# Row maxima and attention output turned by VectorE in 32x32 blocks, and a third bank for the scores

## The chip, the cores and the metric

The kernel runs on one core of a Trainium2 chip. The metric is the device time of one execution in microseconds; before the change it is 676.68 us, the median of 3 runs (676.61 to 677.33). The core has TensorE (PE in the rows), VectorE (DVE), ScalarE (ACT), GpSimd (POOL) and SyncE (SP). Each has its own instruction stream and waits on semaphores; DMAs are issued from the streams of SyncE (SPq) and ScalarE (ACTq).

## The reference

The input is x, 8 images of 16 by 16 tokens with 192 channels, float32. It goes through two transformer blocks with window attention and then two Fourier blocks. The two attention blocks differ in weights, in epsilon and in the Gelu's name only:

```
h = layernorm(x)
win = window_partition(pad(h), 14)            # a 16x16 image becomes 4 windows of 196 tokens, three of them mostly padding
q, k, v = split(win @ qkv_w + qkv_b)          # 12 heads of 16 channels
attn = (q * 16**-0.5) @ k.T + rel_h + rel_w   # rel_*: q with tables of relative positions
out = softmax(attn) @ v                       # 196x196 for each head and window
x = x + unpartition(out @ proj_w + proj_b)
x = x + gelu(layernorm(x) @ w1 + b1) @ w2 + b2   # 192 -> 768 -> 192
```

Each Fourier block takes a 2D transform of the tokens, mixes channels in 8 blocks of 24 with a complex two-layer perceptron, applies a soft threshold of 0.01 and transforms back; it is not touched by the change except through the order of the instructions.

## The kernel before

A job is a pair of images in one attention layer: 4 pairs times 2 layers, 8 jobs n. A job has 512 tokens (TOK): two full windows of 196 tokens (HALF = 98 is half of one) and 120 tokens (CUT) of the cut windows of both images, which are handled together. The heads of a job are gone through in 9 units u of four heads each: u // 3 is the group of four heads, u % 3 the window, where 0 and 1 are the full windows and 2 is the cut tokens. Heads of units are numbered i = 4u + e, 0 to 35.

The order in time is written out by hand, one stream for each engine. For each i TensorE computes the scores twice. `scores` (L445) puts queries on the partitions, so that VectorE can reduce along the free axis to the negated row maximum (`row_max`, L974), written to neg_max. It runs 12 heads ahead (EARLY), and alternates between banks 0 and 1. `scores_T` (L485) later computes the transposed scores into banks 2 and 3, with the negated maximum as one more row of the contraction, row NEG of q_aug; ScalarE takes the exponential into PT (`exps`, L1259), and `values` (L501) multiplies with v_aug into bank 4, which holds both the outputs and, in column HD of each head, the sums.

The maximum has to get from partitions (queries) into one row of q_aug. Before the change, for each unit: TensorE transposes neg_max into bank 5 (`transpose_max`, L471), VectorE copies it to negT with a rounding CAST (`copy_max`, L987), and ScalarE issues the DMAs into q_aug (`send_max`, L1302), two of them for windows 0 and 1, one for window 2. In unit u the sends of unit u+2 stand behind the third exponential; those of units 0 and 1 stand behind the Gelu of the job before. `scores_T` waits for them at the first head of each unit, through neg_in.

The output of each group of heads is copied by ScalarE to o_nat (`copy_o`, L1270), transposed by TensorE into bank 5 (`transpose_o`, L521), divided by VectorE into o_tok (`divide`, L996), transposed back by TensorE into banks 2 and 3 (`transpose_out`, L532), copied to yT by VectorE and ScalarE (`copy_oT`), and projected (`project_out`, L540) with two products of K = 96 a tile.

Between the heads the engines work on the next job's front: its x is transposed and placed (`place_x`), and queries, keys, relative-position terms and values are computed, in banks 6 and 7. Its first 12 `scores` stand in the perceptron of this job (`up`, `down`), through `early_scores`. In the last job the first two Fourier blocks take the place of the next job's front.

Of the kernel before, what the change touches and what calls it, by code (L numbers as in the profile page):

```python
# [23 lines left out]
G = 2  # L24
# [30 lines left out]
def window(u):  # L55
    return u % 3
# [36 lines left out]

def front_bank(n, use):
    return 6 + FRONT.index((n, use)) % 2
# [32 lines left out]
def program(nc, d, x_all, bank, consts):  # L128
    with ExitStack() as ctx:
# [10 lines left out]
        w_proj = [sb(f"w_proj{l}", [96, G, C]) for l in range(2)]  # L140
# [19 lines left out]
        inv_sum = sb("inv_sum", [128, 2, TILES, 4])  # L160
        o_tok = sb("o_tok", [128, TILES, C])
        yT = sb("yT", [128, 2, TOK])
        spare = sb("spare", [1, 2])
# [7 lines left out]
        with ExitStack() as first:  # L171
# [16 lines left out]
                 "k_mm k_hi k_lo p_mm p_hi p_lo r_tok rt_copy r_mm r_hi r_lo v_mm v_copy s_mm max nt_mm negT st_mm exp pv "  # L188
                 "o_copy ot_mm inv_sum o_tok oT_mm oT_dve oT_act proj x1 x1b x2_mm x2_dve x2_act up gelu down out "
# [3 lines left out]
                   xT_dve=1, xT_act=1, q_mm=2, q_hi=2, q_lo=2, q_nat=2, k_mm=2, k_hi=2, k_lo=2, r_tok=4, rt_copy=4, r_mm=4, r_hi=4, r_lo=4,  # L193
                   v_mm=3, v_copy=3, s_mm=HEADS, max=HEADS, nt_mm=UNITS, negT=UNITS, st_mm=HEADS, exp=HEADS,
                   pv=UNITS, o_copy=UNITS, ot_mm=3, inv_sum=3, o_tok=3, oT_mm=2, oT_dve=1, oT_act=1, proj=4, x1=4, x1b=1, xb=1,
# [58 lines left out]
        def _(sp):  # L254
# [14 lines left out]
            def load_back(l):  # L269
                load(w_proj[l][:, :, :], d["proj_w"][l].rearrange("(g p) n -> p g n", g=G), ld_back[l])  # L270
# [75 lines left out]
        def _(pe):  # L346
# [4 lines left out]
            def front_free(n, use):  # L351
# [5 lines left out]
                if kind == "x":  # L357
                    need(pe, ["xT_dve", "xT_act"][j], m, 1)
# [22 lines left out]
            def project(n, use, at, c0, first, count, width, done):  # L381
                l, g = layer(n), int(use[1])
                b = bank[front_bank(n, use)]
                for k in range(first, first + count):
                    if k == 0:
                        front_free(n, use)
                        need(pe, "xT_dve", n, 1)
                        need(pe, "xT_act", n, 1)
# [56 lines left out]
            def scores(n, i):  # L445
# [8 lines left out]
                if i >= 2:  # L454
                    need(pe, "max", n, i - 1)
                else:
                    need(pe, "max", n - 1, HEADS - 1 + i)
                b = bank[i % 2]
# [11 lines left out]

            def transpose_max(n, u):  # L471
                need(pe, "max", n, 4 * u + 4)
                if u >= 1:
                    need(pe, "negT", n, u)
                else:
                    need(pe, "negT", n - 1, UNITS)
                rows = CUT if window(u) == 2 else HALF
                if u >= 7:
                    need(pe, "o_tok", n, (u - 4) // 3)
                else:  # L480
                    need(pe, "o_tok", n - 1, 3)
                t_.transpose(bank[5][0:66, 0:rows], neg_max[0:rows, slot(n, u), :], ident[0:rows, 0:rows])\
                    .then_inc(S["nt_mm"], 1)
# [37 lines left out]
            def transpose_o(n, hg):  # L521
                need(pe, "o_copy", n, 3 * hg + 3)
                if hg >= 1:
                    need(pe, "o_tok", n, hg)
                else:
                    need(pe, "o_tok", n - 1, 3)
                need(pe, "negT", n, min(3 * hg + 7, UNITS))
                for t in range(TILES):
                    last = t_.transpose(bank[5][:, 128 * t:128 * t + 128], o_nat[:, hg % 2, 128 * t:128 * t + 128], ident[:, :])
                last.then_inc(S["ot_mm"], 1)  # L530

            def transpose_out(n):  # L532
                need(pe, "o_tok", n, 3)
                need(pe, "exp", n, HEADS)
                for g in range(G):
                    for t in range(TILES):
                        last = t_.transpose(bank[2 + g][0:96, 128 * t:128 * t + 128], o_tok[:, t, 96 * g:96 * g + 96], ident[:, :])
                    last.then_inc(S["oT_mm"], 1)

            def project_out(n, t):  # L540
                l = layer(n)
                if t == 0:
                    need(pe, "oT_dve", n, 1)
                    need(pe, "oT_act", n, 1)
                    pe.wait_ge(ld_back[l], LD_BACK)
                for g in range(G):
                    last = t_.matmul(bank[PROJ_BANK[t]][:, 0:C], yT[0:96, g, 128 * t:128 * t + 128],
                                     w_proj[l][:, g, :], start=(g == 0), stop=(g == 1))
# [86 lines left out]
            def early_scores(n, i):  # L635
                scores(n, i)
                if i % 4 == 0 and i:
                    transpose_max(n, i // 4 - 1)

# [14 lines left out]
            for i in range(EARLY):  # L654
                early_scores(0, i)
# [10 lines left out]
            for n in range(JOBS):  # L666
                more = n + 1 < JOBS
                for u in range(UNITS):
                    for e in range(4):
# [4 lines left out]
                        if e == 1 and u + 2 < UNITS:  # L674
                            transpose_max(n, u + 2)
# [889 lines left out]
```

## Time and profile before

| | |
|---|---|
| median of the runs | 676.68 us |
| profiled execution | 682.86 us |
| its span | 681.1 us |
| TensorE busy | 623.2 us, 92% |
| VectorE busy | 360.6 us, 53% |
| ScalarE busy | 334.0 us, 49% |
| GpSimd busy | 129.9 us, 19% |

Busy time counts computing instructions. Instructions that issue DMAs are not in it; the timeline shows them as ACTq and SPq. A matmul's record includes the time for which its data run through the array, so that records of neighbours overlap. PEclk is the granted clock of TensorE, 1.00 for 2.4 GHz and 0.50 for 1.2 GHz. Jobs out of the middle repeat each 69.0 us (the same exponential starts at 121.03 and 190.03).

### The profile page before, as it was taken

The numbers are of one execution on the slowest core, as the hardware profiler recorded it, in microseconds if no ns is written. First come the engines' busy times: TensorE is split into PE (matmuls) and PEld (weight loads), VectorE is DVE, ScalarE is ACT, GpSimd is POOL, SyncE is SP. The second block draws the span as 40 slices with busy tenths as digits, with TensorE's granted clock in tenths as the row PEclk, the third lists the DMA queues.
The fourth block names the chain that finished last, engine by engine and source line by source line (L and its number), as shares of the span: only waits on it lengthen the run. The fifth ranks groups of instructions, "written<-read, shape, count | busy, mean of one in ns | idle before, by whom it ended". The sixth has DMA issues, their size and how long they took to land.

```text
span 681.1 us, 14753 instructions
## 1 busy us (share of the span) xinstructions
PE 623.2 (92%) x5696; PEld 480.5 (71%) x5696; DVE 360.6 (53%) x989; ACT 334.0 (49%) x807; POOL 129.9 (19%) x172
## 2 busy tenths in 40 slices
PE   3799999999999999999999999999999999899996
PEld 2587776777677768775877587758775876477674
DVE  4447463746374637462655365546552764426665
ACT  3326743674367435744474447543744365315453
POOL 1800032003300330023002400140013000412220
PEclk9959999999999999999999999999999999799998
DMA  4774670067205720571047003700280000000000
GB/s 110 163 154 119 135 168 7 3 133 153 69 2 124 160 59 3 113 157 36 3 87 162 22 2 77 172 22 2 66 184 21 3 3 1 1 24 1 24 24 23
DMA packets 33175, 47.51 MB, mean 70 GB/s; under 512 B 5563, under 2 KB 14331, under 8 KB 33107
## 3 DMA queue, kind: packets, MB, share of 16 engines
q1 hardware_dynamic: 31874, 46.18, 29.5%
q8 instruction: 46, 0.75, 0.5%
q10 hardware_dynamic: 1232, 0.40, 0.2%
q14 instruction: 23, 0.18, 0.1%
HBM read 7.25 MB, written 1.57 MB: 13 GB/s over the span
## 4 chain that ended last, share of the span: by engine, by line
issue 55%; PE 25%; POOL 12%; DVE 4%; ACT 2%; DMA 1%; POOLq 0%; ACTq 0%; SPq 0%; DVEq 0%
POOL xn L821 4%; POOL q_nat L802 3%; PE bank L631 2%; PE bank L580 2%; PE bank L625 2%; PE bank L497 2%; PE bank L516 2%; PE bank L390 2%; PE bank L431 2%; POOL x_all L808 2%; POOL x_all L814 2%; POOL rstd L795 1%; PE bank L467 1%; PE bank L614 1%; PE bank L598 1%
## 5 line engine op out<-in xcount | busy, mean ns | idle before, releaser
L1268 ACT ACTIVATE PT<-bank 98x392 f32<-98x392 f32 (+1 forms) x288 | 136.8, 490 | 134.1 <-PE bank L497 130.0
L983 DVE TENSOR_REDUCE neg_max<-bank 98x2 f32<-98x392 f32 x192 | 106.4, 562 | 116.6 <-PE bank L467 116.1
L497 PE MATMUL bank<-q_aug,k_aug 127*98 127x196 f32 (+1 forms) x672 | 112.9, 264 | 0.9 <-ACT PT L1268 0.3
L467 PE MATMUL bank<-k_aug,q_aug 126*98 126x196 f32 x384 | 87.4, 314 | 11.2 <-DVE neg_max L983 9.6
L497 PEld LDWEIGHTS bank<-q_aug,k_aug 127*98 127x98 f32 (+1 forms) x672 | 88.0, 168 | 10.5 <-ACT PT L1268 5.8
L802 POOL TENSOR_TENSOR q_nat<-st_q 96x392 f32<-96x392 f32 (+2 forms) x48 | 24.9, 546 | 330.9 <-DVE st_q L951 330.9
L580 PE MATMUL bank<-w_down,PT 128*128 128x192 f32 x384 | 74.1, 330 | 7.0 <-ACT PT L1299 7.0
L467 PEld LDWEIGHTS bank<-k_aug,q_aug 126*98 126x98 f32 x384 | 56.1, 169 | 33.7 <-DVE neg_max L983 15.9
L390 PE MATMUL bank<-xT,w_qkv 97*96 97x256 f32 (+2 forms) x272 | 75.5, 393 | 1.8 <-ACT xT L1205 1.4
L580 PEld LDWEIGHTS bank<-w_down,PT 128*128 128x128 f32 x384 | 61.8, 190 | 8.7 <-ACT PT L1299 8.2
L981 DVE TENSOR_REDUCE neg_max<-bank 120x1 f32<-120x318 f32 x96 | 46.5, 485 | 33.5 <-PE bank L463 33.4
L516 PE MATMUL bank<-PT,v_aug 98*32 98x196 f32 (+1 forms) x1344 | 61.8, 307 | 0.0
L1299 ACT ACTIVATE PT<-bank,b_up 128x512 f32<-128x512 f32 x48 | 30.4, 683 | 51.2 <-PE bank L572 51.2
L390 PEld LDWEIGHTS bank<-xT,w_qkv 97*96 97x96 f32 (+1 forms) x272 | 39.7, 169 | 10.5 <-issue 3.1
L971 DVE TENSOR_TENSOR st_r<-bank,st_r 84x392 fp32r<-84x392 f32 (+2 forms) x96 | 26.1, 324 | 39.7 <-ACT st_r L1243 39.6
L516 PEld LDWEIGHTS bank<-PT,v_aug 98*32 98x32 f32 (+1 forms) x1344 | 33.7, 109 | 12.4 <-issue 2.9
L463 PE MATMUL bank<-k_aug,q_aug 126*120 126x318 f32 x96 | 42.3, 443 | 0.0
L431 PE MATMUL bank<-w_qkv,xT 97*98 97x192 f32 (+1 forms) x200 | 40.2, 353 | 0.8 <-DVE st_r L971 0.3
L431 PEld LDWEIGHTS bank<-w_qkv,xT 97*98 97x98 f32 (+1 forms) x200 | 34.8, 182 | 3.2 <-DVE st_r L971 2.7
L1243 ACT ACTIVATE st_r<-bank 84x392 fp32r<-84x392 f32 (+2 forms) x96 | 22.6, 308 | 24.9 <-PE bank L424 24.7
L795 POOL TENSOR_TENSOR rstd<-veps,half_pow 128x2 f32<-128x2 f32 x16 | 11.4, 715 | 116.8 <-DVE veps L908 116.5
L413 PE MATMUL bank<-w_rel,q_nat 96*32 96x84 f32 x1024 | 28.7, 243 | 2.8 <-DVE st_k L956 1.0
(97 smaller groups left out, 968.0 us busy)
## 6 DMA issues: line engine op xcount, KB each, us to landing
q_aug<-st_q SPq DMA_DIRECT2D x64, 192.0 KB
k_aug<-st_k SPq DMA_DIRECT2D x64, 192.0 KB, 5.0
q_aug<-st_r SPq DMA_DIRECT2D x64, 168.0 KB
x_all<-in_x SPq DMA_DIRECT2D x4, 384.0 KB, 5.9
q_aug<-negT ACTq DMA_DIRECT2D x96, 1.5 KB
k_aug<-st_p SPq DMA_DIRECT2D x16, 74.2 KB, 2.3
w_up<-in_w_up SPq DMA_DIRECT2D x2, 576.0 KB, 5.0
w_down<-in_down_w SPq DMA_DIRECT2D x4, 288.0 KB, 5.6
```

What stands on the lines that cost most here:

```text
L390: ins = t_.matmul(b[0:96, m:m + width], w_qkv[l][0:97 - part, part, c0 + 96 * g:c0 + 96 * g + 96], xT[0:97 - part, part, at + m:at + m + w ...
L431: ins = t_.matmul(bank[front_bank(n, use)][0:rows, C * k:C * k + C], xT[0:97 - g, g, c0:c0 + rows], w_qkv[l][0:97 - g, g, 2 * C:3 * C], st ...
L463: last = t_.matmul(b[0:CUT, 0:CUT + PADS], q_aug[0:NEG, h, c:c + m], k_aug[0:NEG, h, c:KEYS], start=True, stop=True)
L467: last = t_.matmul(b[0:HALF, WIN * r:WIN * r + WIN], q_aug[0:NEG, h, c + HALF * r:c + HALF * r + HALF], k_aug[0:NEG, h, c:c + WIN], start= ...
L497: last = t_.matmul(b[0:keys, m * k:m * k + m], k_aug[0:NEG + 1, h, c + keys * k:c + keys * k + keys], q_aug[0:NEG + 1, h, c:c + m], start= ...
L516: last = t_.matmul(bank[4][32 * e:32 * e + 32, c:c + m], v_aug[0:rows, t0 + k, head(i), :], PT[0:rows, i % 8, m * k:m * k + m], start=(k = ...
L580: ins = t_.matmul(bank[DOWN_BANK[t]][:, 0:C], hidden[:, f, 128 * t:128 * t + 128], w_down[l][:, f, :], start=(f == 0), stop=(f == MC - 1))
L802: last = g_.tensor_tensor(y, a, b, ALU.add)
L981: ins = v.tensor_reduce(neg_max[0:CUT, slot(n, u), e:e + 1], b[0:CUT, 0:CUT + PADS], AX.X, ALU.max, negate=True)
L983: ins = v.tensor_reduce(neg_max[0:HALF, slot(n, u), e:e + 5:4], b[0:HALF, 0:2 * WIN] .rearrange("p (r m) -> p r m", r=2), AX.X, ALU.max, n ...
L1268: s.activation(PT[0:rows, i % 8, 0:m], bank[2 + i % 2][0:rows, 0:m], ACT.Exp).then_inc(S["exp"], 1)
L1299: s.activation(hidden[:, f, :], bank[UP_BANK[f]][:, :], ACT.Gelu, bias=b_up[layer(n)][:, f:f + 1])\
```

## The change

The maxima and the output are turned by VectorE, 32 by 32 block by block. For the maxima this leaves, in each block of 32 partitions, the maxima of 32 queries; so the DMAs into q_aug carry at most 32 queries each, 8 for a unit of windows 0 and 1 and 4 for one of window 2. The output is turned, divided and turned back in place, o_nat keeps all three groups of heads, and the projection takes it from there with three products of K = 128, against weights that are laid out with zero rows. TensorE's transposes of both go. Bank 5 becomes the third bank of the scores, from head 12 on. Besides, `place_x` on VectorE is spread over three heads, the down-projection begins before the last Gelu, and some of the next job's queries and early scores move.

```diff
+def score_bank(i):
+    return i % 2 if i < EARLY else (5, 0, 1)[i % 3]
...
-        w_proj = [sb(f"w_proj{l}", [96, G, C]) for l in range(2)]
+        w_proj = [sb(f"w_proj{l}", [128, 3, C]) for l in range(2)]
...
-        neg_max = sb("neg_max", [128, 4, 66])
-        negT = sb("negT", [8, 4, CUT], F32R)
-        o_nat = sb("o_nat", [128, 2, TOK])
+        neg_max = sb("neg_max", [128, 4, 32])
+        negT = sb("negT", [128, 4, 32])
+        o_nat = sb("o_nat", [128, 3, TOK])
+        o_tok = yT[:, 0, :].rearrange("p (b e) -> p b e", e=32)
...
-            return 16 * sum(1 if window(k % UNITS) == 2 else 2 for k in range(U % 4, U + 1, 4))
+            return 16 * sum(4 if window(k % UNITS) == 2 else 8 for k in range(U % 4, U + 1, 4))
...
-                if i >= 2:
+                if i > EARLY:
+                    need(pe, "max", n, i - 2)
+                elif 2 <= i < EARLY:
                     need(pe, "max", n, i - 1)
...
-                for g in range(G):
-                    last = t_.matmul(bank[PROJ_BANK[t]][:, 0:C], yT[0:96, g, 128 * t:128 * t + 128],
-                                     w_proj[l][:, g, :], start=(g == 0), stop=(g == 1))
+                for hg in range(3):
+                    last = t_.matmul(bank[PROJ_BANK[t]][:, 0:C], o_nat[:, hg, 128 * t:128 * t + 128],
+                                     w_proj[l][:, hg, :], start=(hg == 0), stop=(hg == 2))
...
-                if t == 0 and f == 0:
-                    need(pe, "gelu", n, MC)
+                if t == 0 and f != 1 and f != 2:
+                    need(pe, "gelu", n, max(3, f + 1))
...
-                        if e == 1 and u + 2 < UNITS:
-                            transpose_max(n, u + 2)
-                        if e == 2 and u >= 4 and u % 3 == 1:
-                            transpose_o(n, u // 3 - 1)
...
-                        if more and f in (1, 4):
-                            early_scores(n + 1, 4 + 2 * t + f // 4)
+                        if more and f in (3, 5):
+                            scores(n + 1, 4 + 2 * t + f // 4)
...
                 ins.then_inc(S["max"], 1)
-            def copy_max(n, u):
-                need(dve, "nt_mm", n, u + 1)
+                if e == 3:
+                    turn_max(n, u)
+
+            def turn_max(n, u):
+                need(dve, "max", n, 4 * u + 4)
...
-                v.tensor_copy(negT[0:rows, slot(n, u), 0:m], bank[5][0:rows, 0:m]).then_inc(S["negT"], 1)
+                v.transpose(negT[:, slot(n, u), :], neg_max[:, slot(n, u), :]).then_inc(S["negT"], 1)
...
             def divide(n, hg):
+                need(dve, "o_copy", n, 3 * hg + 3)
+                need(dve, "oT", n, hg)
+                v.transpose(o_tok[:, :, :].rearrange("p b e -> p (b e)"), o_nat[:, hg, :]).then_inc(S["o_turn"], 1)
+                need(dve, "o_turn", n, hg + 1)
+                v.reciprocal(inv_sum[:, :], o_tok[:, :, HD]).then_inc(S["inv_sum"], 1)
                 need(dve, "inv_sum", n, hg + 1)
+                v.tensor_tensor(o_tok[:, :, 0:HD], o_tok[:, :, 0:HD], inv_sum[:, :].unsqueeze(2).to_broadcast([128, 16, HD]), ALU.mult)\
+                    .then_inc(S["o_div"], 1)
+                need(dve, "o_div", n, hg + 1)
+                v.transpose(o_nat[:, hg, :], o_tok[:, :, :].rearrange("p b e -> p (b e)")).then_inc(S["oT"], 1)
...
-                            if (u, e) == (0, 1):
-                                place_x(n + 1)
+                            if u == 0 and e:
+                                place_x(n + 1, e - 1)
...
-                if window(u) == 2:
-                    act.dma_start(q_aug[NEG:NEG + 1, h:h + 4, c:c + m].bitcast(F32), negT[0:4, slot(n, u), 0:m].bitcast(F32))\
-                        .then_inc(neg_in[slot(n, u)], 16)
-                else:
-                    for r in range(2):
-                        act.dma_start(q_aug[NEG:NEG + 1, h:h + 4, c + HALF * r:c + HALF * r + HALF].bitcast(F32),
-                                      negT[4 * r:4 * r + 4, slot(n, u), 0:HALF].bitcast(F32))\
-                            .then_inc(neg_in[slot(n, u)], 16)
+                for q in range(4):
+                    if window(u) == 2:
+                        k = min(32, CUT - 32 * q)
+                        act.dma_start(q_aug[NEG:NEG + 1, h:h + 4, c + 32 * q:c + 32 * q + k].bitcast(F32),
+                                      negT[32 * q:32 * q + 4, slot(n, u), 0:k]).then_inc(neg_in[slot(n, u)], 16)
+                    else:
+                        k = min(32, HALF - 32 * q)
+                        for r in range(2):
+                            at = c + HALF * r + 32 * q
+                            act.dma_start(q_aug[NEG:NEG + 1, h:h + 4, at:at + k].bitcast(F32),
+                                          negT[32 * q + 4 * r:32 * q + 4 * r + 4, slot(n, u), 0:k])\
+                                .then_inc(neg_in[slot(n, u)], 16)
...
-                copy_oT(n)
```

## Rows read from the trace of the kernel before

**Rows 1.** The page, busy time of each engine over the span
```profile
PE 623.2 (92%) x5696; PEld 480.5 (71%) x5696; DVE 360.6 (53%) x989; ACT 334.0 (49%) x807; POOL 129.9 (19%) x172
```
**Rows 2.** Windows: length, busy of PE, PEld, DVE, ACT, POOL, then PEclk
```profile
190.60:212.60 22.00, 20.87 (x277) 16.80 (x277) 15.00 (x35) 14.97 (x37) 1.57 (x3) 1.00 0.07 19
```
**Rows 3.** Tile negT: duration in ns least/median/longest of each line
```profile
L1311 ACTq DMA_DIRECT2D q_aug<-negT x96: 580/580/1183, 41.9 to 557.3; - x96
L1307 ACTq DMA_DIRECT2D q_aug<-negT x24: 580/581/592, 52.6 to 561.7; - x24
```
**Rows 4.** Timeline of ScalarE, a middle job: start, us taken, engine, line
```profile
188.79 0.50 ACT L1268 ACTIVATE PT<-bank 98x392 f32<-98x392 f32 x1 [8.64 <-PE bank L497]
...
190.63 0.58 ACTq L1307 DMA_DIRECT2D q_aug<-negT  x1
...
194.24 1.19 ACTq L1311 DMA_DIRECT2D q_aug<-negT  x2
195.48 0.50 ACT L1268 ACTIVATE PT<-bank 98x392 f32<-98x392 f32 x1 [0.86 <-PE bank L497]
...
211.97 0.58 ACTq L1307 DMA_DIRECT2D q_aug<-negT  x1
```
**Rows 5.** Timeline of ScalarE, the last job
```profile
537.66 0.58 ACTq L1307 DMA_DIRECT2D q_aug<-negT  x1
...
540.28 1.50 ACTq L1311 DMA_DIRECT2D q_aug<-negT  x2
541.83 0.29 ACT L1319 ACTIVATE xf<-bank 64x144 f32<-64x144 f32 x1 [1.06 <-issue]
...
546.75 0.33 ACT L1284 ACTIVATE o_nat<-bank 128x196 f32<-128x196 f32 x1
546.96 0.50 ACT L1268 ACTIVATE PT<-bank 98x392 f32<-98x392 f32 x1
...
556.66 1.20 ACTq L1311 DMA_DIRECT2D q_aug<-negT  x2
557.91 0.58 ACT L1329 ACTIVATE over<-bank,neg_lambda 72x384 f32<-72x384 f32 x1 [0.78 <-issue]
...
561.66 0.58 ACTq L1307 DMA_DIRECT2D q_aug<-negT  x1
```
**Rows 6.** Timeline of TensorE, the middle job
```profile
192.22 0.42 PE L467 MATMUL bank<-k_aug,q_aug 126*98 126x196 f32 x2 [1.13 <-DVE neg_max L983]
...
195.08 0.35 PE L497 MATMUL bank<-q_aug,k_aug 127*98 127x196 f32 x2
```
**Rows 7.** Timelines of TensorE and ScalarE behind the attention, middle job
```profile
156.63 1.08 PE L537 MATMUL bank<-ident,o_tok 128*96 128x128 f32 x8
157.55 0.60 PE L424 MATMUL bank<-ident,rt 128*84 128x128 f32 x4
158.44 2.84 PE L547 MATMUL bank<-w_proj,yT 96*128 96x192 f32 x16 [0.29 <-issue]
...
178.69 0.92 PE L580 MATMUL bank<-w_down,PT 128*128 128x192 f32 x4 [1.00 <-ACT PT L1299]
...
180.58 5.96 ACTq L1311 DMA_DIRECT2D q_aug<-negT  x4
```
**Rows 8.** Windows around the low granted clock, columns as in Rows 2
```profile
30.00:33.00 3.00, 1.37 (x64) 1.21 (x64) 0.40 (x2) 0.90 (x2) 3.00 (x3) 0.92 0.83 163
37.00:49.00 12.00, 10.84 (x40) 9.42 (x38) 5.22 (x15) 1.85 (x7) 0.00 (x0) 0.50 0.66 144
582.00:584.40 2.40, 0.13 (x2) 0.02 (x1) 2.27 (x12) 0.00 (x0) 1.16 (x2) 1.00 0.00 0
585.00:590.00 5.00, 3.98 (x22) 3.09 (x20) 2.68 (x7) 1.93 (x3) 3.90 (x6) 0.55 0.00 0
```
**Rows 9.** Timeline of TensorE: the same products at the low and the high level
```profile
38.98 2.77 PE L431 MATMUL bank<-w_qkv,xT 97*98 97x192 f32 x8
161.56 1.47 PE L431 MATMUL bank<-w_qkv,xT 97*98 97x192 f32 x8
```

More of the change, by code:

```diff
@@ L469, in scores @@
                 last.then_inc(S["s_mm"], 1)
[L471 to L483, printed above, removed]
             def scores_T(n, i):
@@ L654, in _ @@
             for i in range(EARLY):
-                early_scores(0, i)
+                scores(0, i)
                 if i == 3:
@@ L710, in _ @@
                     mix_in(1, 1)
-                if more:
-                    queries_in(n + 1, 1, 2, 2)
                 for k in range(3):
@@ L737, in _ @@
                     values_in(n + 1, 0)
-                    early_scores(n + 1, 0)
-                    early_scores(n + 1, 1)
+                    scores(n + 1, 0)
+                    scores(n + 1, 1)
                 else:
@@ L751, in _ @@
                     if more and p:
-                        early_scores(n + 1, p + 1)
+                        scores(n + 1, p + 1)
                 if not more:
@@ L938, in normalise, with place_x @@
                 last.then_inc(S["xn2"], 1)
-            def place_x(n):
+            def place_x(n, k):
                 l = layer(n)
-                need(dve, "xT_mm", n, 1)
-                need(dve, "v_mm", n - 1, 3)
-                dve.wait_ge(ld_front[l], LD_FRONT)
-                for dst, src in pieces(xT[0:96, 0, 0:TOK], bank[front_bank(n, "x0")][0:96, :]):
-                    last = v.tensor_scalar(dst, src, affine[l][0:96, 0, 0:1], affine[l][0:96, 1, 0:1], ALU.mult, ALU.add)
-                last.then_inc(S["xT_dve"], 1)
+                if k == 0:
+                    need(dve, "xT_mm", n, 1)
+                    need(dve, "v_mm", n - 1, 3)
+                    dve.wait_ge(ld_front[l], LD_FRONT)
+                dst, src = pieces(xT[0:96, 0, 0:TOK], bank[front_bank(n, "x0")][0:96, :])[k]
+                v.tensor_scalar(dst, src, affine[l][0:96, 0, 0:1], affine[l][0:96, 1, 0:1], ALU.mult, ALU.add)\
+                    .then_inc(S["xT_dve"], 1)
             def q_low(n, g):
@@ L976, in row_max @@
                 need(dve, "s_mm", n, i + 1)
-                b = bank[i % 2]
+                b = bank[score_bank(i)]
                 if e == 0 and UNITS * n + u >= 4:
-                    need(dve, "nt_mm", n, u - 3)
+                    need(dve, "negT", n, u - 3)
                 if window(u) == 2:
@@ L1071, in _ @@
             normalise_first()
-            place_x(0)
+            for k in range(3):
+                place_x(0, k)
             norm_stats(1)
@@ L1272, in copy_o @@
                 need(act, "pv", n, u + 1)
-                if u % 3 == 0:
-                    if hg >= 2:
-                        need(act, "ot_mm", n, hg - 1)
-                    else:
-                        need(act, "ot_mm", n - 1, 3 - hg)
-                p = pieces(bank[4][:, :], o_nat[:, hg % 2, :])
+                if u == 0:
+                    need(act, "proj", n - 1, 4)
+                p = pieces(bank[4][:, :], o_nat[:, hg, :])
                 if window(u) == 2:
```

96 lines of the change are left out of this document (28 added, 68 removed).

## The prediction

> **What bounds the kernel now.** I read the page's busy shares first: the reader is to see one engine near full, TensorE with 92%, and no other above 53% [rows 1]. The page's chain of waits names mostly "issue" (55%), which says only that engines ran their own streams, so I went to the timelines of one job out of the middle, engine by engine, and cut it by windows. In the stretch of 22.0 us in which one job's exponentials and its row-maximum transfers alternate, TensorE is busy 20.87 us and ScalarE 14.97 us [rows 2]. ScalarE looks idle for a third of it. But the busy columns leave out the instructions that issue DMAs, and this change multiplies exactly these. So the view that decides is ScalarE's timeline with the ACTq rows in it.
>
> Every issue of a row-maximum transfer takes 580 ns at the least and in the median, whether it moves 4x98 or 4x120 values [rows 3]; two in a row take 1.19 us, 0.60 us each [rows 4]. Does ScalarE compute meanwhile? What had been handed to it before, yes: the single issue at 190.63 [rows 4] lies beside a running copy. What stands behind it in the program, no. In the last job there is work behind the issues that is ready early. The pair that starts at 540.28 ends at 541.78, and the copy behind it starts at 541.83 after 1.06 us of idle time put down to "issue", not to TensorE; the pair at 556.66 ends at 557.86, and the next instruction starts at 557.91 after 0.78 us of the same [rows 5]. Four pairs show this. In the middle jobs it is unseen because TensorE is slower than the pair: the exponential at 195.48 starts right behind the pair's end at 195.43, and TensorE's product for it (195.08 + 0.35) ends there as well [rows 4, 6]. So the cover is just used up, with two issues.
>
> **The change part by part.** *Sends.* A unit of window 0 or 1 sends 8 pieces in place of 2, a unit of window 2 sends 4 in place of 1: 60 issues a job in place of 15. They stay on ScalarE's stream, behind the third exponential of a unit. In the attention stretch stand the sends of units 2 to 8: 4+8+8+4+8+8+4 = 44. A train of 8 takes 7 x 0.60 + 0.58 = 4.78 us, one of 4 takes 2.38 us; four and three of them are 26.26 us.
>
> *What lies between two trains.* Behind a train's end T, ScalarE runs the fourth exponential (T+0.05, its 0.50 us as in [rows 4]), the copy of o, which delays the next by 0.21 us (start 546.75 to start 546.96 [rows 5]), the first exponential of the next unit at T+0.65, ended T+1.15. TensorE could run ahead only by two heads (two banks of transposed scores): the product for the second waits for T+0.55, the one for the third for T+1.15 and takes 0.35 us [rows 6]. So the third exponential is handed over at about T+1.6, and the next train begins. The first gap has no copy of o: 1.4. Six gaps are 1.4 + 5 x 1.6 = 9.4 us. TensorE's work for a unit is some 3.6 us (21.9 us for six steps between the issues at 190.63 and 211.97+0.58 [rows 4]) and fits beneath 4.78+1.6, and nearly beneath 2.38+1.6. From first issue to last end: 26.3 + 9.4 = 35.7 us in place of 21.9: **+13.8 us a job**.
>
> *Ahead of that stretch.* The sends of units 0 and 1 stand behind the Gelu: now 4 issues from 180.58 on [rows 7], with the exponentials waiting for TensorE until 188.79 [rows 4]. Now 16 issues, 9.6 us, from about 180.0 (negT is ready earlier, the turning follows the reduction at once) to 189.6: the first exponential is 0.9 us late, but the first train begins when the third one is handed over, 190.6 as before, since today's issue at 190.63 waited for its CAST. Cost 0. It also means that what TensorE gains in the down-projection (1.00 us of waiting for the Gelu [rows 7]) leads to an earlier stop, not an earlier start: worth 0.
>
> *Behind that stretch.* TensorE has run ahead by one head; it gains 0.6 us. A transpose of 128 columns holds it for 0.115 us (eight from 156.63 to 157.55 [rows 7]): four of o that go here are 0.46 us. At the end of attention go another four (0.46), the eight of the output (0.92) and 0.29 us of wait; four more projection products come at 2.84/8 = 0.335 us, 1.34 us [rows 7]. But the projection now follows a chain on VectorE: turn, reciprocal, multiply, turn back. The turn is not in the trace; nearest rows are a 128x16 reciprocal 0.25, a 128x512 pass over a bank 0.81; bounds 0.25 and 0.81, I take 0.6 us (the 96x512 copy took 0.69). So the projection starts some 0.7 us before today's 158.44 at best, and the transposes of y wait for VectorE's normalisation as today. All of it: -0.8 us a job (bounds -2.5 and +1).
>
> *The third bank.* It removes TensorE's 1.13 us wait for the reduction behind the placing of x (192.22 [rows 6]); in that place a train now sets the pace: worth 0. The turning of the maxima replaces a CAST of 0.24 us by about the same on VectorE: 0, bounds -1 and +1 us a job; VectorE has slack as soon as ScalarE sets the pace.
>
> *First and last job.* In the first the sends stand between the copies of v; 12 issues more are 7.2 us, mostly beside TensorE's start-up work: I take +2 us, bounds 0 and +7. In the last job the stretch is 537.66 to 562.24, 24.6 us [rows 5]; its gaps hold a further 0.5 to 0.6 us of Fourier work each, 12.4 us, plus 26.3 = 38.7, and it begins 0.2 us earlier: +13.9.
>
> Sum at full clock: 7 x (13.8 - 0.8) + 13.9 - 0.8 + 2 = **+106 us**. The profiled execution took 682.86 us (span 681.1, 1.8 us around it), 6.2 us above the median of 676.68; the sum is added to the median: 783 us.
>
> *TensorE's clock.* Its 92% becomes 50 to 60% in the new stretch: behind a train's start it has about 2.7 us of work, then waits. The granted clock is at 2.4 GHz in nearly the whole run; it stands at 1.2 GHz after two stretches: from about 32.5 on, where TensorE had been busy 1.37 of 3 us, and from about 585.5 on, where it had been idle for most of 582 to 584.4 [rows 8]. In this kernel such pauses would come in each of the four long trains. So I expect falls, and work to bring it back in between. What it costs: eight products of the values took 2.77 us at the low level and 1.47 at the high one [rows 9], nearly twice (1.9). A unit's 3.6 us becomes about 6.5: level with a long train's period (I take +0.5 for its gap), 2.5 us over a short one's 4.0. All low: 4 x 0.5 + 2 x 2.5 + 3 for the unit behind the last train = 10 us a job, 80 us; never low: 0. Nothing puts it nearer to either end, so I take half, +40 us: **822 us**.
>
> The Trainium skill (DMA: Bandwidth & Descriptors, "Issuing engines are not separate DMA queues") says that starting a DMA costs the sequencer a time usually small beside the transfer, and its section on the anatomy of a DMA gives about 50 ns for the dispatch. By that, 60 issues would be an estimated 3 us a job and the first rival below would come out; this trace has 580 ns as the median and the least of 120 issues, and goes against it.
>
> **The rivals.**
> (a) Issues don't decide, TensorE does. It would hold if short pieces were issued in some 0.1 us, since a train must stay below today's pair (1.2 us) to hide. Then what TensorE is rid of counts: 1.13 + 1.00 of waits, 9 transposes of maxima at about 0.05, 12 x 0.115, 0.92, 0.29, less 1.34 and less 0.7 of waiting on VectorE's chain: -3.1 us a job, 652 us, faster. For it: two engines below 55% busy. Against: 4x98 and 4x120 cost the same 580 [rows 3], and the idle times of [rows 5].
> (b) Trains decide, the clock stays high: 783 us. For it: TensorE's pause of 1.13 us leaves the level at 1.00 [rows 2, 6]. Against: the pauses here are as long as the one at 582.
> (c) Trains decide and the low level lasts into the work between two attentions, as it lasted from 37 to 49 with TensorE 90% busy [rows 8]: a further 6 us a job beside the 10: 783 + 128 = 911 us.
>
> **How the numbers follow.** Forecast (822 us) 57%, (b) 26%, (c) 10%, (a) 6%, no change 1%. Unknown issue lengths (580 with 1183 at the most) and the bounds of the tail move the cases by some 15 us. Range 768 to 880: it takes in (b) and leaves out (a), (c) and a little. The likeliest alone: 800 to 850. A difference of 0.2% (1.4 us) is about what a measurement tells from none. Faster 0.06, same 0.01, slower 0.93.
>
> **What would show it.** In the changed profile: ACTq rows with x8 of some 4.8 us, and first exponentials behind them with idle time put down to "issue"; TensorE's share near 75 to 80%, waiting for the exponentials (L1268's successor), not for the maxima; a job of some 82 to 87 us in place of 69; clock digits below 9 in most slices. Wrong would be: issues much shorter than 0.5 us, exponentials that start within a train, or TensorE still over 90%. A clock of 9 throughout would leave (b).

## The result, and the profile after

The changed kernel takes **829.91 us**, the median of 4 runs (828.47 to 832.72), against 676.64 (676.09 to 677.33) for the kernel before in the same session: a ratio of 1.225 (95% interval 1.22 to 1.23). The forecast was 822, its range 768 to 880. The profiled execution took 830.97 us with a span of 829.2, and 682.86 with 681.1 before: 148.1 us of span more.

The page of the kernel after: busy time of each engine, three lines of the span in 40 slices, the chain that ended last, and two groups of instructions (busy, mean ns, then idle time ahead and its releaser).

```profile
PE 695.2 (84%) x5528; PEld 521.4 (63%) x5528; DVE 394.2 (48%) x1029; ACT 324.6 (39%) x799; POOL 129.8 (16%) x172
...
PE   4768999888978998889879897789788966889997
...
ACT  3323533344343443344334333433344333533453
...
PEclk9987699769976997679976999699769989999999
...
issue 57%; PE 17%; POOL 10%; ACTq 7%; ACT 4%; DVE 3%; DMA 1%; POOLq 0%; SPq 0%; DVEq 0%
...
L1225 ACT ACTIVATE PT<-bank 98x392 f32<-98x392 f32 (+1 forms) x288 | 136.4, 491 | 263.7 <-PE bank L489 103.6
L489 PE MATMUL bank<-q_aug,k_aug 127*98 127x196 f32 (+1 forms) x672 | 147.6, 325 | 72.6 <-ACT PT L1225 72.5
```

No engine is near its limit any more: TensorE has fallen from 92% [rows 1] to 84%, and ScalarE, which sets the pace, shows 39%. ACTq, the issuing of DMAs on ScalarE, has come into the chain with 7%. The products of the transposed scores wait 72.5 us for the exponentials, which they had led. The clock digit dips in each attention, in the last one to 8 only.

Tile negT (least, median and longest ns of each line), and ScalarE's timeline in a middle job (start, us taken, what it waited):

```profile
L1265 ACTq DMA_DIRECT2D q_aug<-negT x384: 580/580/1182, 40.1 to 703.3; - x192
L1259 ACTq DMA_DIRECT2D q_aug<-negT x96: 580/580/944, 54.7 to 710.3; - x96
L958 DVE STREAM_TRANSPOSE negT<-neg_max x72: 210/211/214, 35.9 to 701.0; 128x32 f32<-128x32 f32 x72
```
```profile
228.91 0.88 ACT L1225 ACTIVATE PT<-bank 98x392 f32<-98x392 f32 x2 [8.30 <-DVE negT L958]
229.68 0.67 ACT L1162 ACTIVATE xT<-bank,affine 96x392 f32<-96x392 f32 x1
229.93 0.58 ACTq L1259 DMA_DIRECT2D q_aug<-negT  x1
...
230.82 0.50 ACT L1225 ACTIVATE PT<-bank 98x392 f32<-98x392 f32 x1
...
233.79 4.85 ACTq L1265 DMA_DIRECT2D q_aug<-negT  x8
238.69 0.50 ACT L1225 ACTIVATE PT<-bank 98x392 f32<-98x392 f32 x1 [4.41 <-issue]
...
240.90 4.85 ACTq L1265 DMA_DIRECT2D q_aug<-negT  x8
245.80 0.47 ACT L1225 ACTIVATE PT<-bank 106x360 f32<-106x360 f32 x1 [4.43 <-PE bank L489]
...
267.23 2.42 ACTq L1259 DMA_DIRECT2D q_aug<-negT  x4
269.70 0.50 ACT L1225 ACTIVATE PT<-bank 98x392 f32<-98x392 f32 x1 [1.98 <-PE bank L489]
...
277.40 0.47 ACT L1225 ACTIVATE PT<-bank 106x360 f32<-106x360 f32 x1 [1.18 <-PE bank L489]
```

An issue is still 580 ns, for a third or a quarter of the values [rows 3], and for the last piece of a full window, which has only 4x2, as well; there are 480 in place of 120. An issue can start before the instruction ahead of it in the program: the one at 229.93 stands behind the third exponential, which starts at 230.82. A train of eight lasts 4.85 us, and the exponential behind it starts 0.05 us after its end. The names of the releasers are less sure than the times: the idle time at 238.69 is put down to "issue" and the like one at 245.80 to TensorE, yet both end right behind a train. The turning of the maxima, 0.21 us, is nothing beside it.

All kernels of this study can be cut in the same way, at the first and last exponential of an attention and the first and last Gelu. In us, middle job (the third; the sixth for "best"):

```
                     attention   to Gelu   Gelus   to next exponential   clock in attention
before                 31.20      20.26     7.39         10.16              1.00
after                  48.96      20.75     7.38          9.80              0.72
after, best job        47.22      20.74     7.39          9.81              0.82
```

One job takes 86.9 us in place of 69.0 here; in the mean of the first seven 87.5 in place of 69.3.

### The profile page after: what moved, and what is told of

It is laid out like the page before. It is cut to its first block, busy times and chain, and to the rows that moved or that the text cites. A ratio compares the mean times of both kernels' runs of the same rounds, so it can differ in the third digit from the quotient of the medians.

```text
span 829.2 us, 14716 instructions
## 1 busy us (share of the span) xinstructions
PE 695.2 (84%) x5528; PEld 521.4 (63%) x5528; DVE 394.2 (48%) x1029; ACT 324.6 (39%) x799; POOL 129.8 (16%) x172
## 3 DMA queue, kind: packets, MB, share of 16 engines
HBM read 7.54 MB, written 1.57 MB: 11 GB/s over the span
## 4 chain that ended last, share of the span: by engine, by line
issue 57%; PE 17%; POOL 10%; ACTq 7%; ACT 4%; DVE 3%; DMA 1%; POOLq 0%; SPq 0%; DVEq 0%
ACTq L1265 6%; POOL xn L782 3%; POOL q_nat L763 2%; PE bank L599 2%; PE bank L605 2%; PE bank L394 2%; PE bank L489 2%; ACT PT L1225 2%; POOL x_all L769 1%; POOL x_all L775 1%; POOL rstd L756 1%; PE bank L572 1%; ACTq L1259 1%; PE bank L521 1%; PE bank L554 1%
## 5 line engine op out<-in xcount | busy, mean ns | idle before, releaser
L489 PE MATMUL bank<-q_aug,k_aug 127*98 127x196 f32 (+1 forms) x672 | 147.6, 325 | 72.6 <-ACT PT L1225 72.5
L489 PEld LDWEIGHTS bank<-q_aug,k_aug 127*98 127x98 f32 (+1 forms) x672 | 113.5, 217 | 102.7 <-ACT PT L1225 84.1
L473 PE MATMUL bank<-k_aug,q_aug 126*98 126x196 f32 x384 | 92.9, 332 | 1.9 <-DVE neg_max L945 1.1
L394 PE MATMUL bank<-xT,w_qkv 97*96 97x256 f32 (+2 forms) x272 | 92.5, 453 | 1.8 <-ACT xT L1162 1.4
L508 PE MATMUL bank<-PT,v_aug 98*32 98x196 f32 (+1 forms) x1344 | 83.3, 389 | 2.9 <-ACT o_nat L1238 2.9
L473 PEld LDWEIGHTS bank<-k_aug,q_aug 126*98 126x98 f32 x384 | 63.0, 190 | 29.2 <-issue 16.3
L508 PEld LDWEIGHTS bank<-PT,v_aug 98*32 98x32 f32 (+1 forms) x1344 | 43.3, 135 | 21.7 <-ACT PT L1225 6.4
L394 PEld LDWEIGHTS bank<-xT,w_qkv 97*96 97x96 f32 (+1 forms) x272 | 44.5, 195 | 12.2 <-issue 5.6
L417 PE MATMUL bank<-w_rel,q_nat 96*32 96x84 f32 x1024 | 34.4, 276 | 7.4 <-DVE st_k L918 5.2
L521 PE MATMUL bank<-w_proj,o_nat 128*128 128x192 f32 x192 | 33.2, 330 | 4.3 <-DVE o_nat L971 4.3
```

The lines of the kernel that those rows point to most:

```text
L394: ins = t_.matmul(b[0:96, m:m + width], w_qkv[l][0:97 - part, part, c0 + 96 * g:c0 + 96 * g + 96], xT[0:97 - part, part, at + m:at + m + w ...
L473: last = t_.matmul(b[0:HALF, WIN * r:WIN * r + WIN], q_aug[0:NEG, h, c + HALF * r:c + HALF * r + HALF], k_aug[0:NEG, h, c:c + WIN], start= ...
L489: last = t_.matmul(b[0:keys, m * k:m * k + m], k_aug[0:NEG + 1, h, c + keys * k:c + keys * k + keys], q_aug[0:NEG + 1, h, c:c + m], start= ...
L508: last = t_.matmul(bank[4][32 * e:32 * e + 32, c:c + m], v_aug[0:rows, t0 + k, head(i), :], PT[0:rows, i % 8, m * k:m * k + m], start=(k = ...
L521: last = t_.matmul(bank[PROJ_BANK[t]][:, 0:C], o_nat[:, hg, 128 * t:128 * t + 128], w_proj[l][:, hg, :], start=(hg == 0), stop=(hg == 2))
```

## The experiments

**One part alone: the cut.** The kernel before, with each transfer cut by columns; maxima and output still go over TensorE.

```diff
-    for r in range(2): act.dma_start(q_aug[.., at:at + HALF], negT[.., 0:HALF])
+    for q in range(4):
+        for r in range(2): act.dma_start(q_aug[.., at + 32 * q: ..+ k], negT[.., 32 * q:32 * q + k])
```

> The kernel before with one edit: each transfer of maxima is cut by columns into pieces of 32, so 8 issues for a unit of windows 0 and 1 and 4 for window 2, as in the change, and nothing else of it. Theory (the issues hold ScalarE's stream, 0.60 us each): 106 us at full clock and some 45 us from the lower granted clock, 820 to 840 us. Rival (what costs is the turning on VectorE, the third projection product or the third bank): about 677 us.

Measured: 842.45 us (840.98 to 844.15), ratio 1.239 (1.232 to 1.246). The cut alone makes more than the whole loss. Its attentions last 47.5 to 51.3 us (the last one 59.0); the rest of the change gives back some 12 us, mostly behind the Gelu (11.8 to 12.1 us to the next exponential, against 9.8).

**The change without the cut.** The kernel after, with 15 issues a job again. It leaves out the maxima of the queries beyond the first 32 columns (zeros are sent).

```diff
-    for q in range(4): for r in range(2): act.dma_start(q_aug[32 columns], negT[32 * q + 4 * r ..])
+    for r in range(2): act.dma_start(q_aug[98 columns], negT[4 * r:4 * r + 4, .., 0:98])
```

> The changed kernel with 2 issues and 1 issue a unit as before the change. Each carries 98 or 120 columns of negT, of which only the first 32 are maxima and the rest are zeros: the other queries' maxima are left out. The instructions are otherwise those of the change. Theory: without the issues what TensorE is rid of counts: 645 to 665 us, 652 by the first rival's sum. Rival (turning, projection, bank): 800 us and more.

Measured: 674.83 us (672.03 to 679.57, 10 runs), ratio 0.992 (0.989 to 0.996). That the issues are the loss is confirmed, but of the expected gain most is missing: a job out of the middle takes 1.1 us less than before, and the one at the change of layers (the fourth) 2.1 us more, 72.9 in place of 70.8. The segments say where it went: attention 31.07, to Gelu 20.76, to the next exponential 8.70 us. Attention is no shorter without TensorE's wait of 1.13 us for the maxima [rows 6]. TensorE waits here in its place (timelines of TensorE and of ScalarE, kernel with few issues):

```profile
185.66 0.40 PE L489 MATMUL bank<-q_aug,k_aug 127*98 127x196 f32 x2 [1.01 <-ACT PT L1226]
186.22 0.64 PE L394 MATMUL bank<-xT,w_qkv 97*96 97x256 f32 x2 [0.17 <-DVE xT L909]
```
```profile
183.89 1.25 ACT L1163 ACTIVATE xT<-bank,affine 96x392 f32<-96x392 f32 x3
185.02 0.88 ACT L1226 ACTIVATE PT<-bank 98x392 f32<-98x392 f32 x2
```

The output costs more than it frees (TensorE, then VectorE, behind that attention's last exponential, which ends at 213.32):

```profile
217.83 0.82 PE L417 MATMUL bank<-w_rel,q_nat 96*32 96x84 f32 x32 [0.51 <-DVE st_k L919]
...
219.94 4.17 PE L521 MATMUL bank<-w_proj,o_nat 128*128 128x192 f32 x24 [0.72 <-DVE o_nat L972]
```
```profile
217.69 0.70 DVE L965 STREAM_TRANSPOSE yT<-o_nat 128x512 f32<-128x512 f32 x1
218.42 0.25 DVE L967 RECIPROCAL inv_sum<-yT 128x16 f32<-128x16 f32 x1
218.71 0.42 DVE L969 TENSOR_TENSOR yT<-yT,inv_sum 128x256 f32<-128x256 f32 x1
219.17 0.71 DVE L972 STREAM_TRANSPOSE o_nat<-yT 128x512 f32<-128x512 f32 x1
```

The projection starts 219.94 - 213.32 = 6.62 us behind the exponential, before 158.44 - 150.99 = 7.45, so 0.83 earlier, and takes 4.17 us in place of 2.84, 1.33 more: +0.5 us. The wait of 0.51 us has its own lesson. Before, four transposes of o stood in that place (timeline of TensorE, kernel before):

```profile
223.31 0.60 PE L529 MATMUL bank<-ident,o_nat 128*128 128x128 f32 x4
223.95 1.76 PE L413 MATMUL bank<-w_rel,q_nat 96*32 96x84 f32 x64
```

By these rows they covered the way of the keys over ScalarE and VectorE; with them gone, TensorE waits there for nearly as long as they took. Only the early down-projection gains.

**Half the cut.** The same with 30 issues a job, pieces of 49 or 60 columns.

```diff
-    one issue for each r
+    for q in range(2): one issue for each r, of half the columns
```

> The kernel of e2_few_issues with each transfer cut in two by columns: 4 issues for a unit of windows 0 and 1 and 2 for window 2; as there, only the first 32 queries of each transfer carry maxima, the rest zeros. Theory: up to 1.2 us of issues a unit hide beneath TensorE's 3.4 us for it, more does not: a train of 4 with its gap is 2.42 + 1.65 = 4.1 us, 0.6 us over, in four units a job, some 20 us in all: 690 to 700 us. Rival (each issue costs the same from the first on, (830 - 675) / 45 per job = 0.43 us): 15 more a job are 675 + 8 x 15 x 0.43 = 727 us.

Measured: 709.13 us (705.26 to 712.89), ratio 1.044 (1.040 to 1.050), above the theory by 9 us or more and below the rival. The first seven attentions last 34.9 to 37.0 us. The loss is not proportional: 15 issues a job more cost 709.1 - 674.8 = 34 us, the next 30 cost 829.9 - 709.1 = 121. For each issue of a job that is 2.3 us, then 4.0: my reading is that a train of 4 (2.41 us) is partly covered by work that TensorE has, that of a train of 8 the further part isn't, and that the clock adds to it (0.91 to 1.00 in these attentions, 0.66 to 0.82 in after's).

**Same issues, no trains.** The kernel after, with the pieces dealt out over the four exponentials of a unit. Those of units 0 and 1 stay in a row behind the Gelu.

```diff
-    if e == 2 and u + 2 < UNITS: send_max(n, u + 2)
+    if u + 2 < UNITS: send_max(n, u + 2, (e,))
```

> The changed kernel, the same 60 issues a job, but those of the attention stand two by two behind each exponential of a unit (one by one for window 2) instead of all behind the third. Theory (the sequencer is held, the datapath goes on with what it has): exponential and pair of issues overlap, a head takes 1.25 us, a unit with 8 issues 5.0 in place of 6.4 us, one with 4 is set by TensorE again; some 7 us a job, and the clock falls less: 755 to 780 us. Rival (what counts is the number of issues and the chain between them, wherever they stand): 820 us or more.

Measured: 756.93 us (754.93 to 759.46), ratio 1.116 (1.111 to 1.120): as the theory had it. Timeline of ScalarE:

```profile
214.44 1.19 ACTq L1265 DMA_DIRECT2D q_aug<-negT  x2
215.67 0.50 ACT L1225 ACTIVATE PT<-bank 98x392 f32<-98x392 f32 x1 [0.76 <-PE bank L489]
215.70 1.19 ACTq L1265 DMA_DIRECT2D q_aug<-negT  x2
216.93 0.50 ACT L1225 ACTIVATE PT<-bank 98x392 f32<-98x392 f32 x1 [0.77 <-PE bank L489]
```

Now an exponential comes each 1.26 us: the pair's 1.19, 0.03 ahead of it and 0.04 behind. The pair at 215.70 starts 0.03 us behind the exponential at 215.67 and runs beside its 0.50 us: an issue doesn't wait for the end of the instruction ahead of it. The first seven attentions take 39.8 to 42.0 us. Of the 155 us between 15 issues and 60 in trains, 756.9 - 674.8 = 82 are left: about half of the loss thus stays with the count of issues, and the other half goes when they no longer stand in a row. That half holds some of the clock too, which is 0.83 to 0.92 in these attentions; that TensorE can't run ahead beside a row is the reading, not shown by itself.

**The clock.** The kernel after, with 11 products more of 128x112 on TensorE in each of four units, to fill its pauses.

```diff
+    if i in FILLED:    # 4u + 15 for u = 1, 2, 4, 5
+        for k in range(11): t_.matmul(b[:, 400:512], ident, ident[:, 0:112], start=True, stop=True)
```

> The changed kernel with 11 more products on TensorE (identity, into unused columns of the bank that is filled next) ahead of the scores behind the long trains of units 1, 2, 4 and 5, where it waits for ScalarE. Their results are used by nothing. Theory (trains and clock add up): the pauses are filled by some 2.1 us, the granted clock stays high for more of the time, and the time falls although work is added: 780 to 805 us. Rival (the trains alone set the time, the clock costs nothing beside them): 829 us or a little more. Rival (the low clock is most of the loss): below 760 us.

Measured: 851.72 us, the median of 4 runs from 828.39 to 867.04, so scattered that single jobs say more than the total. The theory's 780 to 805 is missed: the mean clock rose from 0.86 to 0.88 to between 0.89 and 0.95, and even the fastest run, the one with 0.95, is only level with after's 829.91. In the profiled execution (846.77 us, clock 0.92) low stretches also lie outside the attention. Windows (length, busy of PE, PEld, DVE, ACT, POOL, PEclk) of after, attention and the rest of the job, and of this kernel, one job at the high level and the attention and rest of the next:

```profile
228.91:277.87 48.96, 40.42 (x358) 29.66 (x356) 21.14 (x48) 21.32 (x59) 1.55 (x3) 0.72 0.19 41
277.87:315.80 37.93, 35.58 (x269) 27.19 (x270) 20.25 (x61) 12.86 (x28) 11.59 (x12) 1.00 0.41 101
```
```profile
326.40:373.62 47.22, 41.52 (x450) 32.87 (x448) 21.41 (x50) 21.38 (x60) 1.56 (x3) 1.00 0.20 45
...
414.99:464.45 49.46, 44.09 (x446) 34.23 (x444) 21.13 (x48) 21.16 (x59) 1.57 (x3) 0.92 0.20 47
464.45:506.69 42.24, 41.24 (x270) 31.26 (x270) 20.19 (x61) 12.99 (x28) 11.69 (x12) 0.85 0.22 55
```

What it gives is an estimate of the price of the clock. One attention ran at 1.00 throughout and took 47.22 us, as the best of after did at 0.82. So of 49.3 us, the mean of after's first seven, the low level makes about 2.1, if the added products cost nothing at 1.00. Where the level fell they seem to cost: the others of this kernel's first seven attentions have 0.86 to 0.93 and still take 48.1 to 52.4 us. In the rest of the job, where TensorE is near full, it is dear: 42.24 us at 0.85 in place of 37.93 at 1.00, where after stands.

**Another queue.** The kernel after, with the same pieces issued by SyncE.

```diff
+    for u in range(2, UNITS): send_max(n, u)      # on SyncE: sp.dma_start(...)
...
-    if e == 2 and u + 2 < UNITS: send_max(n, u + 2)     # on ScalarE
```

> The changed kernel with the same pieces, 60 a job, issued from SyncE's stream in place of ScalarE's. Theory (it is ScalarE's stream that is held): exponentials run freely, 650 to 675 us; SyncE needs 26.3 us for 44 issues in an attention of some 29 us, so one or two units may wait a little for their maxima. Rival (so many small transfers are slow as such, wherever they are issued): near 830 us, with TensorE waiting for the landing.

Measured: 726.01 us (720.25 to 730.70), ratio 1.067 (1.059 to 1.076). ScalarE is free of the issues, and two thirds of the loss are gone, so that the rival is refuted; but the theory's 650 to 675 is missed by 50 us, since SyncE issues no faster. Its timeline, and two of the waits (us in total, times, longest):

```profile
211.40 9.86 SPq L323 DMA_DIRECT2D q_aug<-negT  x16
```
```profile
PEld bank L513 <- DMA q_aug<-negT: 45.4, 29, 6.8
...
PE bank L513 <- DMA q_aug<-negT: 37.4, 25, 6.6
```

16 issues in 9.86 us are 0.62 each (a single one takes 573 ns in the median); the pieces arrive late, and TensorE waits for them.

**The output turned alone.** The kernel after, with the maxima as before: TensorE, bank 5, two banks for the scores, 15 issues; ScalarE's placing of x spread too.

```diff
-    return i % 2 if i < EARLY else (5, 0, 1)[i % 3]
+    return i % 2                                   # and transpose_max, copy_max as before
```

> The changed kernel with the maxima as before it: TensorE's transpose into bank 5, CAST, 2 issues or 1; scores in two banks. The output is turned by VectorE, the down-projection starts early, and besides VectorE's ScalarE's placing of x is spread over three heads too. Theory: down-projection 1.4 us a job less, the wait behind the placing of x 1.1 less, the output's transposes in the attention 0.9 less, queries moved there 0.5 more, the tail 0.5 more: 2.4 us a job, 655 to 663 us. Rival (the third bank was what the change needed): 670 us or more.

Measured: 681.51 us (679.39 to 684.14), ratio 1.005 (1.003 to 1.008): a miss. Attention 31.80, to Gelu 20.75, Gelu to exponential 8.94 us, 68.9 a job in all. The output's +0.5 is in it again; at the change of layers (fourth job) attention and the way to Gelu take 33.16 + 23.92 us, against 31.74 + 21.53 before. Of these 3.8 us, 2.3 are waits of TensorE for VectorE (0.73 for st_k, 1.57 for st_p), of the kind that stands in the kernel with few issues at 217.83; the rest wasn't followed, and the granted clock is 0.93 there. The attention of 31.80 us stands against 31.07 of the kernel with few issues, which has the third bank and the turned maxima.

**The change without any turning.** The kernel before, with the early down-projection and both placings of x spread over three heads.

```diff
-    if t == 0 and f == 0: need(pe, "gelu", n, MC)
+    if t == 0 and f != 1 and f != 2: need(pe, "gelu", n, max(3, f + 1))
...
-    if (u, e) == (0, 1): place_x(n + 1)                 # on VectorE and on ScalarE
+    if u == 0 and e: place_x(n + 1, e - 1)
```

> The kernel before with the small edits alone: the down-projection begins before the last Gelu, two early scores move with it, and the placing of x is spread over three heads on VectorE and ScalarE. Nothing is turned by VectorE. Theory (turning the output gains nothing, the projection's third product takes back what the transposes give): 1.4 + 1.1 us a job, 655 to 661 us, level with e8_output_turned_alone. Rival (turning the output is a gain of its own): 5 us or more behind it.

Measured: 669.10 us (667.89 to 672.88), ratio 0.987 (0.984 to 0.990), the lowest median of all versions. Attention 31.3, to Gelu 20.26, Gelu to exponential 8.94. It isn't level with the version before it but 12 us faster: turning the output, with the queries moved for it, costs time instead of gaining any. The expected 655 to 661 is missed too, since the spread placing of x brought nothing (attention 31.3, before 31.2).

**Which of the two edits.** The kernel before with the down-projection's edit alone (and the two early scores that move with it):

> The kernel before with one edit of the change: the down-projection begins at the third hidden tile instead of the sixth, and the two scores of the next job that stand in it move from f = 1, 4 to f = 3, 5. The placing of x stays in one go. Theory: from the end of the last Gelu to the next first exponential 10.16 us fall to about 8.9 us in each of seven jobs, attention stays at 31.2 and the tail at 20.3, so about 7 x 1.2 = 8.6 us less, 668 to 670 us; the spread placing in the best version so far (669.1 us) was worth nothing. Rival: the spread placing had a share in those 8.4 us, and this kernel takes 671 to 675 us.

Measured: 670.79 us (667.20 to 672.36), ratio 0.989 (0.986 to 0.993); segments 31.20, 20.27, 7.39 and 8.93. The total alone doesn't decide, as it lies between the theory's 668 to 670 and the rival's 671 to 675. The segments do: 10.16 - 8.93 = 1.23 us a job, seven times, is the gain, nothing else in the middle jobs has changed, and the intervals of this and of the version before it overlap. Timeline of TensorE, where [rows 7] had 1.00 us of waiting:

```profile
176.66 1.49 PE L580 MATMUL bank<-w_down,PT 128*128 128x192 f32 x8
177.84 0.48 PE L467 MATMUL bank<-k_aug,q_aug 126*98 126x196 f32 x2
```

And the kernel with few issues, with ScalarE's placing of x spread, to test my reading of its wait of 1.01 us:

```diff
-    if (u, e) == (0, 1): place_x(n + 1)                 # on ScalarE
+    if u == 0 and e: place_x(n + 1, e - 1)
```

> The kernel with few issues (674.8 us; it leaves out the maxima of the queries beyond the first 32 columns of a unit) with one more edit: ScalarE places the next job's x one piece behind each of exponentials 1, 2 and 3 instead of all three pieces behind exponential 1. Theory: TensorE's wait of 1.01 us at its ninth group of scores, which stands in each job of that kernel, comes from exponential 2 standing behind those three pieces (1.25 us), so each of seven attentions falls from 31.07 to about 30.1 us and the kernel to some 668 us. Rival: TensorE is held there by its own work or by the row maxima as well, another wait of about the same length takes the place, and attention stays at 31.0 to 31.3 us, the kernel at 673 to 676.

Measured: 674.73 us (671.74 to 678.45), attention 31.08. The rival is right. The same 1.18 us of waiting have only changed names:

```profile
185.53 0.40 PE L489 MATMUL bank<-q_aug,k_aug 127*98 127x196 f32 x2 [0.43 <-ACT PT L1227]
186.67 0.64 PE L394 MATMUL bank<-xT,w_qkv 97*96 97x256 f32 x2 [0.75 <-DVE xT L909]
```

The queries behind it need the placed x, and TensorE is at that point early by as much, whichever row carries the wait. What would shorten this place stays open.

## Why the prediction was right, step by step

*What decides.* Right: the view with the ACTq rows, not the busy shares. The cut alone gives 842 us, its removal 675.

*Sends.* A train of 8 was put at 4.78 us and takes 4.85, one of 4 at 2.38 and takes 2.41. The gaps were put at 1.4 and five times 1.6; in the best job of after (clock 0.82) they are 1.45, 1.72, 1.65, 1.67, 1.72 and 2.21. From the first issue to the last end it takes 37.4 us in place of 35.7, and 37.45 in the job of filled pauses that stood at 1.00: **+15.4 a job, not +13.8**.

*Ahead of the stretch.* Put at 0, in truth -1.2: from the last Gelu to the first issue 229.93 - 219.09 = 10.84 us, before 190.63 - 178.63 = 12.00. The 16 sends take 9.77 us (9.6 predicted) and then set the first exponential. But they start at 219.05, at the last Gelu's very end, and not 1.4 us behind it as put; and the first train then begins while x is still being placed.

*Behind the stretch.* This is the step whose sign was wrong: -0.8 predicted (its terms, with the 0.7 of waiting that (a) names, give -0.7); measured +1.4 from the last train to the last exponential (47.22 - 1.02 - 37.36 = 8.84 against 7.44), and +0.5 to the Gelu. I had counted what TensorE is rid of. The trains don't make this loss: the kernel with the cut alone has the same trains, and in its sixth job 7.32 us there (7.2 to 9.2 in the others) and 20.26 to the Gelu. The kernel with few issues has 8.02 and 20.75 without any long train. What these two differ in is the turned output and the moved queries, for which no term stood: four groups of the next job's queries stand among the last unit's scores in place of two. TensorE, then ScalarE, after, sixth job:

```profile
538.50 0.67 PE L394 MATMUL bank<-xT,w_qkv 97*96 97x256 f32 x2
538.82 0.59 PE L489 MATMUL bank<-q_aug,k_aug 127*106 127x120 f32 x3
539.25 0.62 PE L394 MATMUL bank<-xT,w_qkv 96*96 96x256 f32 x2
...
539.46 0.47 ACT L1225 ACTIVATE PT<-bank 106x360 f32<-106x360 f32 x1 [1.18 <-PE bank L489]
```

Before, third job:

```profile
219.32 1.49 PE L390 MATMUL bank<-xT,w_qkv 96*96 96x256 f32 x6
...
219.52 0.47 ACT L1268 ACTIVATE PT<-bank 106x360 f32<-106x360 f32 x1 [0.49 <-PE bank L497]
```

The last unit's four exponentials take 2.75 us before and in the kernels without the turned output, 3.5 in six of after's first seven jobs. So some 0.6 to 0.8 of the 1.4 us comes with the new order of TensorE's work; the rest wasn't separated. The +0.5 to the Gelu comes with the VectorE chain of the turned output and the third product. The terms of the projection themselves were sized well: 0.8 us earlier (0.7), 1.33 longer (1.34), a turn of 0.70 us (0.6).

*Sum at the high level.* -1.2 + 15.4 + 1.4 + 0.5 = +16.1 a job, where 13.0 had been put: 3.1 us too little, 22 us in seven jobs.

*The clock.* +40 us was taken, 5 a job, half of 0 to 80 for want of a measure. Attention takes 47.22 us at 1.00 (with the added products) and 49.28 in the mean of after: an estimate of **2.1 a job**, 15 us in seven where 35 had been put. The clock falls as foreseen (0.66 to 0.82 in these attentions); that it costs less than put fits a unit that ScalarE paces and that has room for slower products. The last job takes 19.7 us more (attention 56.50 in place of 37.11, and 0.3 behind it), of which its +5 for the clock had made 18.1; its share of the clock wasn't separated. The terms close: 7 x 16.1 + 15 + 19.7 + 0.7 for the start are 148 us, and the spans differ by 148.1. But they close because the clock's share is the difference between after's mean job and its best one, so the sum doesn't test it. The two errors, 22 us too little for the stretches and 20 too much for the clock, nearly cancelled: that 822 came so near to 830 is luck.

*First job.* +2 predicted. Before's profiled execution had a low clock there (0.67 from 25.00 to its first exponential at 50.76), after's hadn't (0.93, and 51.44); kernels with 15 or 30 issues and a clock of 0.92 to 1.00 there have their first exponential at 45.2 to 46.5. So it is some +5 to +6, within the bound of 7, and hidden in the comparison of the two profiles.

*Third bank and turning of maxima.* Put at 0; no run takes them out of after alone. Where no train covers them they are worth 0.7 us a job: attention 31.07 in the kernel with few issues, 31.80 in the one with the output turned alone.

*The rivals.* (a), that TensorE decides, is refuted by the 580 ns and by the cut alone. Its sum was off too: -3.1 us a job, where the kernel with few issues shows 67.92 - 69.01 = -1.1, since one wait came back under another name and the output costs 0.5. (b), 783 us, failed on its condition: the clock didn't stay high. With the trains at their true size it would have said 783 + 22 = 805. (c), 911 us, is refuted for this kernel: 1.00 in the rest of the job. The kernel with filled pauses shows that this state exists (0.85, 4.3 us longer).

*The signs.* Trains of 4.85 us (4.8 foreseen), 86.9 us a job (82 to 87), clock digits below 9 in 16 of 40 slices (most had been foreseen), TensorE behind the exponentials. TensorE's share was missed: 84%, not 75 to 80, since at the low level its work takes longer (695 us busy in place of 623).

By the Trainium skill (DMA: Bandwidth & Descriptors, "Issuing engines are not separate DMA queues") the time to start a DMA is usually small beside the DMA itself. No run shows how long these transfers take by themselves, so that comparison stays open; what the runs show is that 0.60 us on ScalarE's stream and 0.62 on SyncE's aren't small for this kernel. The 50 ns that the prediction took from the Trainium skill's section on the anatomy of a DMA stand there for a DMA that GpSimd issues, and ScalarE issues these; so they were no price for them, and 580 ns don't contradict them.

## What to carry to other kernels

Price a DMA issue as an instruction of the stream that it stands in, and read the queue rows of that engine beside its busy share, which leaves them out. Cutting a transfer is paid by the count of pieces, and dearest where they stand in a row in front of the work on which another engine waits; if they must be many, deal them out or give them to a stream that has nothing else to do, up to what that stream can issue (16 in 9.86 us on SyncE). A wait or a piece of work that is removed is worth something only if nothing else ends at the same moment: 1.13 us here came back as 1.18 under two other names. And an edit that comes along with a change is a term of its own: the early down-projection alone gives 1.2 us a job, and the turned output without the third bank takes back nearly all of it (68.9 us a job against 69.0).

## What the runs showed of the hardware

- An issue takes 580 ns on ScalarE, for 4x2, 4x32, 4x98 or 4x120 values alike, and 573 ns on SyncE; in a row 0.60 to 0.62 us each.
- It can start 0.89 us before the instruction ahead of it on ScalarE (229.93 and 230.82), or beside it (0.03 us behind its start), but holds back the one behind it (an exponential starts 0.05 us behind a train's end).
- VectorE's turn in 32 by 32 blocks: 128x32 float32 0.21 us, 128x512 0.67 to 0.71 us.
- More work for TensorE raised the mean granted clock (0.87 to between 0.89 and 0.95) and didn't make the kernel faster (828.39 us at best, against 829.91). A granted clock of 0.85 where TensorE is near full cost 4.3 us of 42.2.
